# Moving half of the rounding of the activation codes into the attention's units

## The chip, the cores and the metric

The kernel runs on one core of one Trainium2 chip. The metric is the device time of one execution in microseconds (us), the median of the runs. The engines are PE (TensorE: matmuls; PEld is its weight load), DVE (VectorE), ACT (ScalarE), POOL (GpSimd) and SP (SyncE, which here only issues DMAs).

## What is computed

A decoder of two layers on x of 16 batches x 128 tokens x 256 channels. The change concerns the second layer's attention, whose queries, keys and values are computed from activations that have been scaled, clamped and rounded to FP8 codes:

```
def _div_clamp_fp8(x, scale):
    y = jnp.clip(x / scale, -448, 448)
    y = y.astype(bfloat16)
    return fp8_roundtrip(y)                       # the codes

q  = LN(codes(ln_out, q_in_scale)  @ wq)          # 16 heads of 128
k  = LN(codes(ln_out, k_in_scale)  @ wk);  v = codes(ln_out, v_in_scale) @ wv
core = softmax(q k / sqrt(d)) v
qx = LN(codes(ln_out, qx_in_scale) @ wqx); kx, vx from ctx_2048
xout = softmax(qx kx / sqrt(d)) vx
out = (codes(concat(core, xout), proj_smooth) @ wproj) * scales
```

So one input, ln_out, is rounded four times, once for each scale: for the queries, the keys, the values of the self attention, and for the queries of the cross attention.

## The kernel before, in words

All activations stay in SBUF. `XT` [128, 2, 2048] holds ln_out transposed: 2 blocks of 128 channels by 2048 tokens (16 batches of 128). `xq` [128, 4, 2, 2048] holds the codes: for each of four scales j (0 queries, 1 keys, 2 values, 3 cross) and each channel block k one *plane* of 2048 tokens.

`quant_layer` (L1464) does two things, one after the other, with a barrier of all engines between them.

`round_codes` (L1477) makes all eight planes, n = 4 x 2. Per plane ACT scales XT into bf16 (L1531, one instruction of 2048 columns), DVE clamps (L1549), takes the power of two out of it (L1554) and makes the rounding constant (L1562), each as two halves of 1024 columns; PE adds y + m - m in PSUM with three bf16 products per tile of 512 columns (L1521 to L1523), four tiles a plane; ACT copies two of the four tiles out (L1541) and DVE the other two (L1579). PE starts with three products of the identity (L1511).

`attention` (L1610) then works off 128 *units*: eight head groups w (four of self, four of cross attention) by 16 batches b, unit n = 16 w + b. The order of the work is written out by hand: each engine runs through the same steps, and in step s it does for each entry (stage, lag) of its list the stage of unit s - lag. Each engine's queue is in order, and semaphores tie them together. The lists are at L1830 (PE), L1907 (ACT), L1979 (POOL) and L2058 (DVE):

```
PE:   queries 0, keys_values 0, turn_p_warm 3, turn_q 1, turn_k 1, output 5, values 3, scores 1, late_output 5
POOL: rounded 5, row_deviation 7, deviation 0, prepare 0, context_low 0, normalise 2
DVE:  row_moments 6, apply_kv 1, maxima 2, query_statistics 0, clamp 4, key_statistics 0, power 4,
      magic 4, reciprocals 2, rounding 4, residual 5, apply_q 0
```

The loop that ties a unit to the next: PE computes queries and keys/values of unit u (L1731 to L1753) into one PSUM bank each; DVE takes their statistics (`query_statistics` L1992, `key_statistics` L1997); POOL adds an epsilon (L1947) and raises to the power -0.5 (L1952); DVE applies that to the queries (`apply_q` L2003) and keys/values (`apply_kv` L2010), which frees the banks; PE's queries of unit u+1 wait for `apply_q` of unit u. The other chains have one or more units of lag: scores (L1779), their maxima (DVE, L2017), exponentials (ACT, L1882), reciprocals (DVE, L2024), `normalise` (POOL, L1956), values (L1797), and the rounding of the result: scaled by ACT (L1899), `clamp`, `power`, `magic`, `rounding` on DVE (L2028 to L2043), `rounded` on POOL (L1963), then the output products (L1808) and DVE's `residual` (L2047).

`prepare` on ACT and POOL splits the weights of the next head group into a high and a low part: POOL has one such subtraction of 512 columns in the steps b = 5, 7, 9, 11 (L1423) and 10, 12 (L1432), and one of an expert's weights at b = 3 and 13 (L1940).

The attention keeps its normalised q, k, v and turned probabilities (`qn`, `kvn`, `pt`) in the space of XT, which nothing reads by then; so they appear as XT in the profile.

## Time and profile before

| | us |
|---|---|
| median of 3 runs | 1412.66 (1412.54 to 1413.17) |
| profiled execution, span | 1411.1 |
| PE busy | 1322.5 (94%) |
| DVE busy | 1073.4 (76%) |
| ACT busy | 944.4 (67%) |
| POOL busy | 909.4 (64%) |
| round_codes, first to last instruction | 341.9 to 370.8 |
| attention, first unit's products to the last unit's queries | 371.6 to 1121.6 |

The times of the runs are those of the whole execution; the profile gives one execution's span, from its first to its last instruction, with nothing of what lies around it. The profile places each instruction at a start with a duration. Shares of the whole span mix stages with different limits, so the stages named in the table are read each by itself.

### The profile page before, as it was taken

How to read it: one execution, taken by the hardware profiler on the slowest of the kernel's cores; microseconds unless marked ns; L12 is line 12 of the kernel's file. 1: busy time of each engine (PE TensorE's matmuls, PEld its weight loads, DVE VectorE, ACT ScalarE, POOL GpSimd, SP SyncE). 2: the span in 40 equal slices, each digit the busy share in tenths (PEclk: the TensorE clock that was granted, in tenths of full speed). 3: DMA queues.
4: the chain of work that ended last, by engine and by line, in shares of the span. 5: the costliest groups of instructions: out<-in, count | busy, mean ns of one | idle time of the engine just before them, and what ended most of it. 6: DMA issues, size and time to landing. Idle time of an engine off the chain costs nothing. (4 is left out here: it accounts for less than half of the span.)

```text
span 1411.1 us, 28423 instructions
## 1 busy us (share of the span) xinstructions
PE 1322.5 (94%) x8507; PEld 1098.8 (78%) x8507; DVE 1073.4 (76%) x2567; ACT 944.4 (67%) x3181; POOL 909.4 (64%) x1101
## 2 busy tenths in 40 slices
PE   9999988896799999999999999999999978999992
PEld 4445666663499999999999989998998855889882
DVE  5899768897788888888998888888888847444443
ACT  3997457776488787888887777777777746332331
POOL 4996237774178687786887767766867844455542
PEclk9999999998999999999999999999999999999996
DMA  9421110000101002002011020020100149577665
GB/s 341 158 117 63 36 46 2 1 2 1 60 1 62 29 2 98 1 31 69 24 61 53 1 91 2 1 91 2 46 1 24 68 144 340 138 168 162 164 162 134
DMA packets 55160, 105.85 MB, mean 75 GB/s; under 512 B 5052, under 2 KB 33668, under 8 KB 52708
## 3 DMA queue, kind: packets, MB, share of 16 engines
q1 hardware_dynamic: 46100, 84.90, 17.5%
q0 software_dynamic: 7488, 10.23, 4.5%
q10 hardware_dynamic: 1424, 8.91, 1.5%
q8 instruction: 73, 1.20, 0.4%
q14 instruction: 75, 0.61, 0.1%
HBM read 75.58 MB, written 28.44 MB: 74 GB/s over the span
## 5 line engine op out<-in xcount | busy, mean ns | idle before, releaser
L1882 ACT ACTIVATE pr_<-ps,neg_ 128x128 f32<-128x128 f32 x512 | 181.3, 366 | 64.5 <-DVE neg_ L2017 64.5
L1899 ACT ACTIVATE y<-ps,invsm 128x128 bf16<-128x128 f32 x512 | 146.4, 369 | 61.5 <-PE ps L1797 61.3
L1952 POOL TENSOR_TENSOR rstd<-var,half 128x6 f32<-128x6 f32 x128 | 172.3, 1346 | 10.1 <-POOL var L1947 0.2
L1963 POOL TENSOR_TENSOR z<-t,m 128x512 fp32r<-128x512 f32 x128 | 148.8, 1163 | 3.3 <-DVE t L2043 3.3
L1947 POOL TENSOR_TENSOR var<-stat,deps 128x6 f32<-128x6 f32 x128 | 26.0, 203 | 184.2 <-DVE stat L1997 184.2
L1779 PEld LDWEIGHTS ps<-qkt 128*128 128x128 f32 x1024 | 134.0, 191 | 10.3 <-ACT qkt L1866 2.7
L1808 PE MATMUL ps<-phi,z 128*128 128x256 f32 x512 | 138.2, 303 | 1.2 <-POOL z L1963 1.2
L1779 PE MATMUL ps<-qkt 128*128 128x128 f32 x1024 | 135.3, 275 | 2.3 <-ACT qkt L1874 2.1
L1797 PE MATMUL ps<-XT 128*128 128x256 f32 x512 | 131.8, 380 | 2.9 <-ACT XT L1890 2.8
L1956 POOL TENSOR_TENSOR pr_<-pr_,rec_ 128x512 f32<-128x512 f32 x128 | 133.5, 1043 | 1.4 <-DVE rec_ L2024 1.4
L1808 PE MATMUL ps<-plo,z 128*128 128x256 f32 x512 | 127.3, 279 | 0.0
L1992 DVE BATCH_NORM_STATS2 stat<-ps 128x6 f32<-128x256 f32 x256 | 97.7, 423 | 29.1 <-PE ps L1732 28.2
L2498 POOL DMA_INDIRECT sums<-f_ys,f_ids x39 | 61.8, 1585 | 88.7 <-PE ps L2354 43.4
L1731 PE MATMUL ps<-whi,xq 128*128 128x512 f32 x256 | 111.4, 435 | 4.7 <-DVE XT L2003 3.2
L1866 ACT ACTIVATE qkt<-ps,aff 128x512 f32<-128x512 f32 x128 | 99.0, 773 | 11.3 <-PE ps L1762 11.3
L1882 ACT ACTIVATION_READ_ACCUMULATOR pr_<-ps,neg_ 128x1 f32 x512 | 103.8, 203 | 0.0
L1732 PE MATMUL ps<-wlo,xq 128*128 128x512 f32 x256 | 100.8, 394 | 0.0
L1890 ACT ACTIVATE XT<-ps 128x512 f32<-128x512 f32 x128 | 76.5, 598 | 36.0 <-PE ps L1788 32.6
L2047 DVE SCALAR_TENSOR_TENSOR X<-ps,pscale,X 128x256 f32<-128x256 f32 x128 | 61.9, 484 | 47.8 <-PE ps L1808 47.6
L1808 PEld LDWEIGHTS ps<-phi,z 128*128 128x128 f32 x512 | 96.4, 188 | 2.2 <-POOL z L1963 1.7
L1808 PEld LDWEIGHTS ps<-plo,z 128*128 128x128 f32 x512 | 97.1, 190 | 0.1
L1797 PEld LDWEIGHTS ps<-XT 128*128 128x128 f32 x512 | 87.3, 189 | 11.2 <-ACT XT L1890 4.4
(357 smaller groups left out, 4023.8 us busy)
## 6 DMA issues: line engine op xcount, KB each, us to landing
f_w_low<-w_low SPq DMA_DIRECT2D x39, 512.0 KB, 3.6
centred<-raw_weights ACTq DMA_DIRECT2D x8, 1024.0 KB, 3.9
w_low<-w_dram SPq DMA_DIRECT2D x8, 1024.0 KB, 10.6
aw_st<-centred SPq DMA_DIRECT2D x7, 1024.0 KB, 6.1
raw_weights<-wself_dram SPq DMA_DIRECT2D x4, 1024.0 KB, 13.8
raw_weights<-wcross_dram SPq DMA_DIRECT2D x4, 1024.0 KB, 15.1
w_rest<-w_dram SPq DMA_DIRECT2D x8, 512.0 KB, 3.9
w_high<-w_top SPq DMA_DIRECT2D x8, 512.0 KB, 2.7
```

The lines of the kernel that those rows point to most:

```text
L1731: pe.matmul(bQ[:, :], x[:, k, :], whi[:, u.slot, 0, k, :], start=(k == 0), stop=False)
L1732: mm = pe.matmul(bQ[:, :], x[:, k, :], wlo[:, u.slot, 0, k, :], start=False, stop=(k == CB - 1))
L1779: mm = pe.matmul(bS[:, h * S:(h + 1) * S], qkt[:, u.par, h, :], qkt[:, u.par, HEADS + h // 2, :], start=True, stop=True)
L1797: mm = pe.matmul(bO[:, two], kvn[:, u.place, 2 + w, :], pt[:, u.par, two], start=True, stop=True)
L1808: mm = pe.matmul(bW[:, 0:C], z[:, u.par, h * S:(h + 1) * S], part[:, u.slot, h // 2, h % 2, :], start=(h == 0 and part is phi), stop=(h == ...
L1866: act.activation(qkt[:, u.par, 0:HEADS, :], bTQ[:, :].rearrange("p (h s) -> p h s", h=HEADS), ACT.Identity, bias=a[:, 1:2], scale=a[:, 0:1 ...
L1882: ins = act.activation(pr[:, u.par, h, :], bS[:, h * S:(h + 1) * S], ACT.Exp, bias=neg[:, u.par, h:h + 1], accum_out=tot[:, u.par, h:h + 1])
L1899: ins = act.activation(y[:, u.par, h * S:(h + 1) * S], bO[:, h * S:(h + 1) * S], ACT.Copy, scale=invsm[:, head:head + 1])
L1952: pool.tensor_tensor(rstd[:, u.par, 0:6], v, half[:, :], ALU.pow).then_inc(s_rstd, 1)
L1956: pool.tensor_tensor(pr[:, u.par, :, :], pr[:, u.par, :, :], rec[:, u.par, :].unsqueeze(2).to_broadcast([P, HEADS, S]), ALU.mult).then_inc ...
L1963: pool.tensor_tensor(z[:, u.par, :], t[:, u.par, :], m[:, u.par, :], ALU.subtract).then_inc(s_z, 1)
L1992: dve.bn_stats(stat[:, u.par, 6 * h:6 * h + 6], two)
```

## The change

Ahead of the attention `round_codes` now makes only the codes of self attention (three scales, six planes) and only of the first eight batches (1024 of 2048 columns, two tiles a plane). DVE's instructions there are 512 columns wide, and DVE and ACT copy out one tile each a plane.

The rest is cut into 20 *late pieces* of 512 columns. Pieces 0 to 5 are the six self planes of batches 8 to 11, pieces 6 to 11 those of batches 12 to 15; each of the units 0 to 11 has one. Pieces 12 to 19 are the cross codes of all batches, in the units 12, 16, ..., 40. A piece is a scaling on ACT, four instructions on DVE (`late_clamp`, `late_power`, `late_magic`, `late_rounding`, the last an addition of two tensors in SBUF) and one subtraction on POOL (`late_rounded`), one step later. PE has no part in a piece. PE's queries of unit 8 wait for six pieces, those of unit 12 for twelve, those of unit 64 for all.

The pieces are worked in buffers that are idle then (`raw_context`, `w2_top`), one each in turn; for that the first half of the first expert's weights is split at b = 12 instead of 3 in head group 0. XT must now live on: it lies on the right side of SBUF, the cross codes are written in its place (`xcross`), and `qn`, `kvn`, `pt` get a buffer of their own (`spare`).

```diff
-        xq = sbuf(ctx, "xq", [P, 4, CB, TOK], F32R)
+        xq = sbuf(ctx, "xq", [P, 3, CB, TOK], F32R)
         with ExitStack() as inner:
             round_codes(inner, xq, quant, **args)
 
-        attention(xq, row_stats, quant, rows_stored, w2_stored, **args)
+        columns_ctx.close()
+        xcross = sbuf(rows_ctx, "xcross", [P, CB, TOK], F32R, side="right")
...
-    N = 4 * CB
-    TILES = TOK // W512
+    N = 3 * CB
+    TILES = EARLY // W512
     BY_ACT = TILES // 2
...
+        def late(u, after):
+
+            at = u.n - after
+            i, off = (at, 0) if at < LATE_SELF else divmod(at + 3 * LATE_SELF, 4)
+            return i if off == 0 and 0 <= i < LATE else None
+
+        def late_place(i):
+
+            if i < LATE_SELF:
+                q, j = divmod(i, 3 * CB)
+                return j // CB, j % CB, slice(EARLY + q * W512, EARLY + (q + 1) * W512)
+            q, k = divmod(i - LATE_SELF, CB)
+            return CROSS, k, slice(q * W512, (q + 1) * W512)
...
-            return slice(0, I) if u.b == 3 else slice(I, 2 * I) if u.b == 13 else None
+            return slice(0, I) if u.b == (3 if u.w else 12) else slice(I, 2 * I) if u.b == 13 else None
...
+                    if u.n == EARLY // S:
+                        pe.wait_ge(s_late_z, 3 * CB)
+                    if u.n == (EARLY + W512) // S:
+                        pe.wait_ge(s_late_z, LATE_SELF)
+                    if u.n == SELF:
+                        pe.wait_ge(s_late_z, LATE)
...
+                    i = late(u, 0)
+                    if i is None:
+                        return
+                    if i >= 2:
+                        act.wait_ge(s_late_z, i - 1 if i < LATE_SELF else i)
+                    late_y, late_m, late_t = late_buffers(i)
+                    j, k, at = late_place(i)
+                    act.activation(late_y, XT[:, k, at], ACT.Copy, scale=quant.inv[:, j, k:k + 1]
...
-                in_steps([(turned_q, 2), (turned_k, 2), (prepare, 0), (context_high, 0), (scaled, 4), (row_normed, 8), (exps, 2),
+                in_steps([(late_scaled, 0), (turned_q, 2), (turned_k, 2), (prepare, 0), (context_high, 0), (scaled, 4), (row_normed, 8), (exps, 2),
...
+                def late_rounded(u):
+                    i = late(u, 1)
+                    if i is None:
+                        return
+                    j, k, at = late_place(i)
+                    late_y, late_m, late_t = late_buffers(i)
+                    pool.wait_ge(s_late_t, i + 1)
+                    pool.tensor_tensor(xcross[:, k, at] if j == CROSS else xq[:, j, k, at], late_t, late_m, ALU.subtract
+                                       ).then_inc(s_late_z, 1)
...
-                in_steps([(rounded, 5), (row_deviation, 7), (deviation, 0), (prepare, 0), (context_low, 0), (normalise, 2)])
+                in_steps([(rounded, 5), (row_deviation, 7), (late_rounded, 0), (deviation, 0), (prepare, 0), (context_low, 0), (normalise, 2)])
...
+                    dve.tensor_scalar(late_y, late_y, FP8_MAX, -FP8_MAX, ALU.min, ALU.max).then_inc(s_late_clamp, 1)
...
+                    dve.tensor_scalar(late_m.bitcast(U16), late_y.bitcast(U16), 0x7F80, None, ALU.bitwise_and
+                                      ).then_inc(s_late_p2, 1)
...
+                    dve.tensor_scalar(late_m, late_m, FP8_MIN_NORMAL, ROUND, ALU.max, ALU.mult).then_inc(s_late_m, 1)
...
+                    dve.tensor_tensor(late_t, late_y, late_m, ALU.add).then_inc(s_late_t, 1)
...
-                          (magic, 4), (reciprocals, 2), (rounding, 4), (residual, 5), (apply_q, 0)])
+                          (late_clamp, 0), (magic, 4), (late_power, 0), (reciprocals, 2), (late_magic, 0), (rounding, 4),
+                          (residual, 5), (late_rounding, 0), (apply_q, 0)])
```

What the tables do to the queues shows best in a unit in the middle of the first twelve. DVE, one unit of head group 0, from the maxima of one step to `apply_q`; before:

```order
L2017 TENSOR_REDUCE neg_<-ps 128x4
L1992 BN_STATS stat<-ps 128x6 x2
L2028 TENSOR_SCALAR y<-y 128x512
L1997 BN_STATS stat<-ps 128x6
L2034 TENSOR_SCALAR m<-y 128x512
L2039 TENSOR_SCALAR m<-m 128x512
L2024 RECIPROCAL rec_<-tot 128x4
L2043 TENSOR_TENSOR t<-y,m 128x512
L2047 SCALAR_TENSOR_TENSOR X<-ps,pscale,X 128x256
L2003 TENSOR_TENSOR XT<-ps,rstd 128x512
```

and in the changed kernel (its line numbers; the four rows on `raw_context` are the late piece):

```order
L2081 BN_STATS stat<-ps 128x6 x2
L2117 TENSOR_SCALAR y<-y 128x512
L2086 BN_STATS stat<-ps 128x6
L2123 TENSOR_SCALAR m<-y 128x512
L2047 TENSOR_SCALAR raw_context<-raw_context 128x512
L2128 TENSOR_SCALAR m<-m 128x512
L2055 TENSOR_SCALAR raw_context<-raw_context 128x512
L2113 RECIPROCAL rec_<-tot 128x4
L2064 TENSOR_SCALAR raw_context<-raw_context 128x512
L2132 TENSOR_TENSOR t<-y,m 128x512
L2136 SCALAR_TENSOR_TENSOR X<-ps,pscale,X 128x256
L2072 TENSOR_TENSOR raw_context<-raw_context 128x512
```

All four late instructions stand between the key statistics and `apply_q` (L2092, which follows), the addition last of all. POOL in the steps of units 11 and 12, with the weights' subtractions that are due there; before:

```order
L1947 TENSOR_TENSOR var<-stat,deps 128x6
L1952 TENSOR_TENSOR rstd<-var,half 128x6
L1423 TENSOR_TENSOR wlo<-aw_st,whi 128x512
L1956 TENSOR_TENSOR pr_<-pr_,rec_ 128x512
L1963 TENSOR_TENSOR z<-t,m 128x512
```

and in the changed kernel, to the start of unit 13:

```order
L2008 TENSOR_TENSOR rstd<-var,half 128x6
L1426 TENSOR_TENSOR wlo<-aw_st,whi 128x512
L2012 TENSOR_TENSOR pr_<-pr_,rec_ 128x512
L2019 TENSOR_TENSOR z<-t,m 128x512
L1971 TENSOR_TENSOR xq<-w_top 128x512
L2003 TENSOR_TENSOR var<-stat,deps 128x6
L2008 TENSOR_TENSOR rstd<-var,half 128x6
L1435 TENSOR_TENSOR plo<-aw_rows,phi 128x512
L1996 TENSOR_TENSOR w_rest<-w_rest,w_top 128x512
L2012 TENSOR_TENSOR pr_<-pr_,rec_ 128x512
L2019 TENSOR_TENSOR z<-t,m 128x512
L1971 TENSOR_TENSOR xcross<-raw_context 128x512
```

The piece's subtraction (L1971) stands behind `rounded` and ahead of the next unit's deviation; unit 12 has two subtractions of weights in one step, where before it had one.

## Rows read from the trace of the kernel before

**Rows 1.** Stretches: busy us (x instructions) of PE, PEld, DVE, ACT, POOL; clock; DMA
```profile
344.00:371.60 27.60, 23.68 (x100) 9.35 (x98) 25.60 (x63) 21.67 (x24) 0.19 (x3) 0.95 0.00 1
371.60:379.00 7.40, 4.37 (x22) 3.76 (x23) 3.25 (x7) 0.00 (x0) 1.55 (x2) 0.91 0.76 283
470.00:530.00 60.00, 60.00 (x444) 57.00 (x444) 52.27 (x125) 49.55 (x164) 46.32 (x49) 1.00 0.01 2
```

**Rows 2.** Timeline of round_codes: start, us, engine, line, instruction [idle before <-releaser]
```profile
346.78 0.43 PE L1523 MATMUL ps<-m,minus 128*128 128x512 bf16 x1
...
354.49 1.28 DVE L1579 CAST xq<-ps 128x512 fp32r<-128x512 f32 x2
355.69 0.75 DVE L1549 TENSOR_SCALAR y<-y 128x1024 bf16<-128x1024 bf16 x2
...
357.70 1.28 DVE L1579 CAST xq<-ps 128x512 fp32r<-128x512 f32 x2
...
369.50 1.34 DVE L1579 CAST xq<-ps 128x512 fp32r<-128x512 f32 x2 [0.68 <-PE ps L1523]
...
371.58 0.50 PE L1731 MATMUL ps<-whi,xq 128*128 128x512 f32 x1 [1.47 <-POOL deps L1915]
```

**Rows 3.** Timeline of one unit of the attention (b = 12), DVE, PE, then POOL
```profile
438.26 0.47 PE L1731 MATMUL ps<-whi,xq 128*128 128x512 f32 x1
440.40 0.43 DVE L1997 BATCH_NORM_STATS2 stat<-ps 128x6 f32<-128x256 f32 x1
440.75 0.28 DVE L2034 TENSOR_SCALAR m<-y 128x512 uint16<-128x512 uint16 x1
441.06 0.29 DVE L2039 TENSOR_SCALAR m<-m 128x512 bf16<-128x512 bf16 x1
441.27 0.17 DVE L2024 RECIPROCAL rec_<-tot 128x4 f32<-128x4 f32 x1
441.39 0.69 DVE L2043 TENSOR_TENSOR t<-y,m 128x512 f32<-128x512 bf16 x1
442.45 0.48 DVE L2047 SCALAR_TENSOR_TENSOR X<-ps,pscale,X 128x256 f32<-128x256 f32 x1 [0.37 <-PE ps L1808]
442.85 0.68 DVE L2003 TENSOR_TENSOR XT<-ps,rstd 128x512 f32<-128x512 f32 x1
443.92 0.47 PE L1731 MATMUL ps<-whi,xq 128*128 128x512 f32 x1
...
441.19 1.35 POOL L1952 TENSOR_TENSOR rstd<-var,half 128x6 f32<-128x6 f32 x1
442.51 1.27 POOL L1432 TENSOR_TENSOR plo<-aw_rows,phi 128x512 fp32r<-128x512 f32 x1
443.74 1.03 POOL L1956 TENSOR_TENSOR pr_<-pr_,rec_ 128x512 f32<-128x512 f32 x1
```

**Rows 4.** Timeline and instructions by line: DVE and POOL at one time
```profile
28.98 2.04 POOL L572 TENSOR_TENSOR kv<-ct 128x512 f32<-128x512 f32 x2
L272 DVE SCALAR_TENSOR_TENSOR n_shift<-n_mean_var,n_rstd x3: 129/164/1000, 29.0 to 137.4; 128x4 f32<-128x4 f32 x3
...
677.49 1.17 POOL L1963 TENSOR_TENSOR z<-t,m 128x512 fp32r<-128x512 f32 x1
677.86 0.94 DVE L2028 TENSOR_SCALAR y<-y 128x512 bf16<-128x512 bf16 x1
...
1130.23 0.66 DVE L2043 TENSOR_TENSOR t<-y,m 128x512 f32<-128x512 bf16 x1
1130.39 1.40 POOL L1956 TENSOR_TENSOR pr_<-pr_,rec_ 128x512 f32<-128x512 f32 x1 [0.55 <-DVE rec_ L2024]
...
L2043 DVE TENSOR_TENSOR t<-y,m x128: 660/693/694, 396.5 to 1145.0; 128x512 f32<-128x512 bf16 x128
```

**Rows 5.** Timeline of the attention's first unit
```profile
376.00 0.69 DVE L2003 TENSOR_TENSOR XT<-ps,rstd 128x512 f32<-128x512 f32 x1 [1.82 <-POOL rstd L1952]
...
376.75 0.50 PE L1731 MATMUL ps<-whi,xq 128*128 128x512 f32 x1 [3.03 <-DVE XT L2003]
```

More of the change, by code:

```diff
@@ L1529, in scaled @@
                     act.wait_ge(s_z, (n - 2) * TILES)
-                for h in (halves if n == 0 else [slice(0, TOK)]):
+                for h in (halves if n == 0 else [slice(0, EARLY)]):
                     act.activation(y[:, n % 3, h], XT[:, n % CB, h], ACT.Copy,
@@ L1655, in attention @@
         d_c = [sem(f"u_dc{k}") for k in range(4)]
+        s_late_y, s_late_clamp, s_late_p2, s_late_m, s_late_t, s_late_z = (
+            sem("u_late_" + n) for n in ("y", "clamp", "p2", "m", "t", "z"))
         names = ("cst", "chi", "clo", "q", "kv", "stat", "var", "rstd", "qn", "kvn", "tq", "tk", "qt", "kt", "sc", "neg",
@@ L1708, in load_context @@
                         sp.wait_ge(s_clo, b - 3)
+                    else:
+                        sp.wait_ge(s_late_z, LATE)
                     sp.dma_start(raw[:, b % 4, :, :], io["ctxT"].rearrange("(k p) n -> p k n", p=P)[
```

66 lines of the change are left out of this document (49 added, 17 removed).

## The prediction

> **What bounds the kernel now.** I read first the busy time by stretches, then the timeline of each of the two stages that the change touches. In the attention's steady stretch PE is busy for all of 60 us at the full clock, and DVE for 52.3 of them [rows 1]: PE sets the pace, with DVE close behind. In the rounding stage DVE is the busiest, 25.6 of 27.6 us [rows 1]. So the change takes work from a stage that DVE bounds and hands it to one in which DVE has about an eighth to spare.
>
> The timeline of one unit shows how little that is. Call K the start of the key statistics (440.40). `apply_q` starts at K+2.45, PE's next queries at K+3.52 [rows 3]. In the first unit, where PE only waits, queries follow `apply_q` by 0.75 (376.00 to 376.75) [rows 5], so they could start at K+3.20: the loop has 0.3 us in hand. DVE itself has a hole of 0.4 ahead of the residual: the rounding ends at 442.08, the residual starts at 442.45 [rows 3]. A unit takes 5.66 us (queries 438.26 to 443.92) [rows 3], and key statistics follow its queries by 2.14.
>
> **What the rounding stage gives back.** A plane costs DVE 3.21 us (354.49 to 357.70): two casts in 1.20, then six instructions of 1024 columns (two each for clamp, power, constant) in 2.01, or 0.335 each [rows 2]. With 512 columns an instruction of this kind starts 0.21 us after the one before (441.06 to 441.27) [rows 3], and a cast takes 0.61 until the next instruction starts (two of them 354.49 to 355.69). A plane becomes 6 x 0.21 + 0.61 = 1.87. The start does not shrink: PE runs its first products at half pace, and the second tile of plane 0 is done at 347.2 [rows 2]. From there DVE does cast 0 (0.61) and four times a plane with the cast before it (7.5): 355.3. The last tile then needs its three products and a cast, which ends at about 356.8. Before, the last cast ended at 370.84 [rows 2]. **Saved: 14.0 us** (12.5 to 15). The 0.75 us of barrier up to the first product (371.58) remain.
>
> **What a late piece costs.** The ACT scaling (about 0.6) and POOL's subtraction (1.17, as its twin in [rows 4]) lie beside other work; DVE's four instructions stand on the loop, between K and `apply_q`. In the queue order: power K+0.35, then at 0.21 each late clamp, magic, late power, reciprocal, then 0.12, late magic, 0.21, rounding at K+1.52, residual at K+2.13, late addition at K+2.53, `apply_q` at K+3.14. Interleaving hides the waits between dependent instructions and fills the hole, so 1.5 us of work would delay `apply_q` by only 0.7, and the queries by 0.7 - 0.3 = 0.4.
>
> But the late addition reads two tensors of SBUF, and there the trace shows something else. An addition of that kind on POOL and DVE hold each other up. POOL's subtraction of 677.49 ends at 678.66; DVE's bf16 clamp issued at 677.86 takes 0.94 instead of the 0.28 of its like at 440.75, and ends 0.15 after it. A two-tensor operation of four elements takes 1.00 instead of 0.13 at 29.0, beside a POOL instruction on two tensors that began at 28.98. The other way round, `normalise` issued at 1130.39, while the rounding's addition ran, takes 1.40 instead of 1.03 [rows 3, 4]. So who comes second waits for the end of the first, and then has all but 0.14 us of its own time before it. The Trainium skill (SBUF — State Buffer, Who interferes with whom) has this as a rule: DVE's second pair of ports is GpSimd's only one, held by an instruction with two SBUF inputs, or a bf16 tensor_scalar in its fast mode, to its end. The rows agree. It speaks against this change.
>
> Where the two meet: POOL is in the power function from K+0.79 to K+2.11, then in `prepare` or `normalise` (442.51) [rows 3]. The power function holds nobody up: the rounding's addition starts 0.2 us into it and takes 0.69, and in all 128 units it never took more than 0.694 [rows 3, 4]. The late addition, however, comes at K+2.53, when POOL has been in its next instruction for 0.4 us:
>
> - Plain unit: `normalise` ends at K+3.15; the addition at 3.15 + 0.55 = K+3.70; `apply_q` 0.08 earlier, queries at K+4.37 instead of 3.52. **+0.9** with the 0.1 that DVE is then late for the next statistics.
> - Unit with a weights' subtraction: that ends at K+3.38, the addition at 3.93. `normalise` now waits for it (to 4.83), then `rounded` (5.95) and the piece's subtraction (7.07). The next unit's clamp, which stands just ahead of its key statistics, would be due at K+6.5 and must wait for it: 7.22, and the key statistics start 0.08 before, at K+7.14 instead of 5.66. **+1.5**.
>
> The sum over the units:
>
> - 0 to 3: nothing. DVE waits there for POOL's power function between the statistics and `apply_q`, and the clamp chain of older units has not begun. If that cover were short: 0.2 each.
> - 4: no residual yet, the addition meets `normalise` head on; 0.3 if it wins, 1.2 if not: 0.8.
> - 5, 7, 9, 10 (with weights): 6.0. 6 and 8: 1.8.
> - 11: the queries of unit 12 wait for piece 11, whose subtraction ends at K+7.07; key statistics of unit 12 at K+9.27: 3.6. Queued behind this wait is everything of PE.
> - 12: two weights' subtractions and a piece; the clamp waits for `rounded`, the power for the piece's subtraction: 1.7, and 0.3 in unit 13 from POOL's late deviation.
> - 16, 20, 24, 32, 36, 40: 6 x 0.9 = 5.4; 28 (with weights): 1.2, as the following unit without a piece catches up.
> - The clock: PE idles 3 us in unit 0, and the granted clock of that stretch is 0.91, a part of it at 1.2 instead of 2.4 GHz [rows 1, 5]. The gap before unit 12 is as long; I take 0.6.
>
> Together **21.4 us**. The moved expert weights are in the unit-12 term; the extra DMA wait of the context (all pieces, done at unit 41) ends before its first use at unit 46, and costs nothing. Bounds: with no stop at all each piece costs 0.4, unit 11 3.2 and units 12 and 13 1.2 together, in all 10; if in addition POOL's power function is held up by the denser bf16 instructions ahead of it (by 0.13, the rest of a `magic`), everything shifts by that in 16 units: 23.5; with 1 us more of POOL backlog around units 9 to 13, 26.
>
> The profiled execution would go from a span of 1411.1 to 1411.1 - 14.0 + 21.4 = 1418.5; the median of the runs lies 1.6 above the span, so **1420.1**.
>
> **Rivals.**
>
> 1. *The order flips.* If POOL falls behind DVE, the late addition gets the ports first, and `normalise` waits instead. Then a piece costs 0.4, and only the clamps after units with weights are stopped (+0.6 each, four times). Cost 10 + 2.4 = 12.4: 1411.0, no change. For it: POOL's chain grows by 1.2 per unit. Against it: its power function starts on the statistics, which DVE itself delivers. Chance 0.12.
> 2. *The pieces are covered*, the other side. The pair of instructions does not collide, being bf16 to fp32 rather than fp32; each piece then costs 0.4, in all 10: 1408.7, faster. It decides if the stop is under 0.2 us a piece. The 1.40 of `normalise` beside just such an addition speaks against it. If the single pieces are absorbed too, 1406. Chance 0.13.
> 3. *Single pieces absorbed.* The eight later ones cost half, because the unit after catches up: cost 18, 1416.6. This is inside my forecast's range (1415 to 1425).
> 4. *The power function blocks as well.* It is a GpSimd instruction that reads SBUF, and all bf16 instructions issued after K+0.79 would wait for K+2.11: late power, late magic, rounding, residual and late addition follow then, 0.3 to 1.3 later than above, say 0.75 in 16 units: 12 more, 1432. The rows speak against it, as the rounding's addition runs through it unhindered [rows 3, 4]. Chance 0.05. The Trainium skill (SBUF — State Buffer, Who interferes with whom) says that whoever starts first holds the pair for the whole instruction, which read to the letter gives this rival; the 0.69 beside the power function disagrees.
> 5. The change does less than it says: no sign of it; the queues show all pieces.
>
> **How the numbers follow.** My forecast has the remaining 0.70. A measurement of this kernel tells about 0.2%, 2.8 us, from no change: 1409.8 to 1415.5. Faster: rival 2 and a little of rival 1: 0.15. Same: most of rival 1 and the low end of the forecast: 0.15. Slower: 0.70. The range leaves out rival 2 in part and rival 4: 1410 to 1427.
>
> **What would show it.** Right: the last cast near 356.8, the first product of the attention at 357.5; late additions of 1.2 to 1.5 us instead of 0.69 in units 5 to 11; clamps of about 1 us in units 6, 8, 10; query starts 6.5 to 7.2 apart in units 5 to 10 and 8.8 to 9.3 from 11 to 12. Wrong: late additions of 0.69 and `normalise` of 1.4 (rival 1), both at their old times (rival 2), late power or magic of over 1 us in the power function (rival 4), or a rounding stage that does not end before 358.

## The result and the profile after

The changed kernel takes **1428.45 us** (median of 4 runs, 1426.95 to 1429.68); the kernel before took 1412.91, measured beside it (4 runs, 1412.54 to 1414.62). The ratio is 1.0106, interval 1.0093 to 1.0118: slower by 15.5 us, where 7.4 were forecast; 1428.45 lies above the forecast's upper end of 1427. The profiled execution has a span of 1426.7 us, against 1411.1.

The times of one and the same kernel here differ by up to 10 us (e5 below), and a good part of that goes with a stretch of half clock in the routing stage behind the attention, whose instructions the change leaves alone (last section). So the kernels are compared mainly by stretches, each read from the one profiled execution of its kernel. The start of a unit is the start of its first query product, and the *distance* of a unit runs from there to the start of the next unit.

| us | first product | units 0 to 3 | 4 | 5 to 10 | 11 | 12 | 13 | 14 to 41 | 42 to 126 | last unit's queries to the end |
|---|---|---|---|---|---|---|---|---|---|---|
| before | 371.58 | 21.76 | 5.30 | 33.96 | 5.66 | 5.66 | 5.66 | 158.48 | 513.01 | 289.99 |
| after | 357.47 | 22.74 | 5.91 | 41.94 | 13.37 | 8.48 | 6.20 | 167.32 | 513.98 | 289.28 |
| difference | -14.1 | +1.0 | +0.6 | +8.0 | +7.7 | +2.8 | +0.5 | +8.8 | +1.0 | -0.7 |

The sum of the differences is the 15.6 us of the spans. The last column's 0.7 lies in stages whose instructions the change leaves alone.

The page of the changed kernel, its busy times:

```profile
span 1426.7 us, 28355 instructions
PE 1319.5 (92%) x8431; PEld 1096.0 (77%) x8447; DVE 1094.8 (77%) x2625; ACT 940.0 (66%) x3189; POOL 939.9 (66%) x1121
```

DVE has 21 us more than before and POOL 31. PE has 3 us less, which is a balance of two parts. Ahead of the attention it is busy for some 12 to 14 us less, mainly because 60 rounding products are gone (a few of its records are missing there). In the attention it is busy for 10.9 us more with the same number of products, in part at half clock. The attention's windows, of the kernel before and of the changed one:

```profile
371.58:1121.07 749.49, 743.81 (x5130) 1.00 0.10 37
357.47:1137.42 779.95, 754.73 (x5130) 0.99 0.10 35
```

The attention is 30.5 us longer, so 19.5 of them are PE's waits and 10.9 are products that last longer.

The windows of the changed kernel, with the columns of [rows 1]: the rounding stage, the attention's first unit, the surroundings of unit 11, and 60 us of units with single pieces:

```profile
344.00:357.00 13.00, 10.27 (x40) 4.18 (x39) 11.22 (x42) 9.00 (x12) 0.00 (x0) 0.92 0.01 1
357.47:364.87 7.40, 4.37 (x20) 3.71 (x21) 4.56 (x11) 1.84 (x3) 2.67 (x3) 0.89 0.75 283
425.00:445.00 20.00, 12.30 (x67) 10.69 (x67) 12.39 (x25) 9.76 (x33) 12.11 (x11) 0.83 0.00 1
456.00:516.00 60.00, 58.51 (x422) 54.27 (x423) 53.91 (x131) 46.95 (x157) 45.25 (x47) 1.00 0.15 54
```

In the third line PE works for 12.3 of 20 us at a granted clock of 0.83. In the last it is busy for 58.5 of 60 where [rows 1] had all 60.

**The rounding stage** ends as forecast. The timeline of the changed kernel (start, duration, engine, line, operation; in brackets the idle time before it and its releaser), last casts and first product of the attention:

```profile
354.62 0.68 DVE L1583 CAST xq<-ps 128x512 fp32r<-128x512 f32 x1
356.06 0.69 DVE L1583 CAST xq<-ps 128x512 fp32r<-128x512 f32 x1 [0.76 <-PE ps L1527]
357.47 0.50 PE L1766 MATMUL ps<-whi,xq 128*128 128x512 f32 x1 [1.46 <-POOL deps L1961]
```

The last cast ends at 356.75 (forecast 356.8), the first product starts at 357.47 (forecast 357.5).

**A late piece meets POOL**, as forecast. The timeline of the changed kernel around the late addition of 425.88, in a unit with a weights' subtraction (L2132 is the rounding's own addition, L2072 the late one, L2012 `normalise`, L2092 `apply_q`):

```profile
424.89 0.69 DVE L2132 TENSOR_TENSOR t<-y,m 128x512 f32<-128x512 bf16 x1
425.59 1.27 POOL L1435 TENSOR_TENSOR plo<-aw_rows,phi 128x512 fp32r<-128x512 f32 x1
425.88 1.53 DVE L2072 TENSOR_TENSOR raw_context<-raw_context 128x512 f32<-128x512 bf16 x1
426.82 1.49 POOL L2012 TENSOR_TENSOR pr_<-pr_,rec_ 128x512 f32<-128x512 f32 x1
427.33 0.68 DVE L2092 TENSOR_TENSOR spare<-ps,rstd 128x512 f32<-128x512 f32 x1
```

The rounding's own addition (L2132) takes 0.69. The late one (L2072), issued 0.29 us into POOL's subtraction, takes 1.53 and ends 0.55 after POOL's 426.86. Then `normalise`, issued while the late addition ran, takes 1.49 instead of 1.03, and `apply_q` (L2092), for which PE's next queries wait, starts at 427.33. All 20 late additions, by instructions of the line (count: shortest/median/longest in ns, first to last start):

```profile
L2072 DVE TENSOR_TENSOR raw_context<-raw_context x14: 684/1288/1529, 361.0 to 615.8; 128x512 f32<-128x512 bf16 x14
L2072 DVE TENSOR_TENSOR w_top<-w_top x6: 693/1516/1524, 367.3 to 433.1; 128x512 f32<-128x512 bf16 x6
```

Put beside POOL's timeline, 15 of the 20 start inside a POOL operation of 512 columns, and those take 1.28 to 1.53; the five that do not take 0.68 or 0.69. Four of these five stand in units 0 to 3. The fifth is that of unit 4, where it is `normalise` that is stopped:

```profile
384.48 0.68 DVE L2072 TENSOR_TENSOR raw_context<-raw_context 128x512 f32<-128x512 bf16 x1
384.58 1.48 POOL L2012 TENSOR_TENSOR pr_<-pr_,rec_ 128x512 f32<-128x512 f32 x1
```

**Unit 11** is where the forecast missed most. The timeline of the changed kernel, from piece 11's subtraction on POOL to unit 12's queries on PE:

```profile
436.61 1.15 POOL L1971 TENSOR_TENSOR xq<-w_top 128x512 fp32r<-128x512 f32 x1
437.80 0.72 ACT L1880 ACTIVATE raw_context<-XT,inv 128x512 bf16<-128x512 f32 x1 [6.51 <-POOL xq L1971]
438.42 0.76 ACT L1912 ACTIVATE qkt<-ps,aff 128x512 f32<-128x512 f32 x1
439.08 0.55 ACT L1920 ACTIVATE qkt<-ps,aff 128x256 f32<-128x256 f32 x1
439.74 2.05 PE L1814 MATMUL ps<-qkt 128*128 128x128 f32 x8 [6.61 <-ACT qkt L1912]
441.44 0.77 PE L1766 MATMUL ps<-whi,xq 128*128 128x512 f32 x1
```

And the waits of the same kernel from 430 to 442 us (what waited, for whom: total, times, longest):

```profile
PE ps L1814 <- ACT qkt L1912: 6.6, 1, 6.6
ACT raw_context L1880 <- POOL xq L1971: 6.5, 1, 6.5
DVE neg_ L2106 <- PE ps L1814: 6.0, 1, 6.0
```

PE does not wait first for its queries' codes. It waits for ACT: `late_scaled` of piece 12 (L1880) is the first entry of ACT's step, and it waits for twelve pieces, so for the end of piece 11 on POOL (`act.wait_ge(s_late_z, i - 1 if i < LATE_SELF else i)`). Its own buffer, `raw_context`, is free once piece 10 has ended; the wait for piece 11 guards `w2_top`, into which the weights' split of b = 12 writes later in the step. Behind it in ACT's queue stand the turned q and k of an older unit (L1912, L1920), for which the scores wait (L1814), and they stand ahead of the queries in PE's order. So the scores, 1.7 us, come after the wait rather than in it. In the granted clock the gap shows too: while PE idles it falls to the lower level, 1.2 GHz, at 438.3, and stays there to 445.2, where the 8 scores take 2.05 instead of 1.05 and the first query product 0.77 instead of 0.47 [rows 3].

### The profile page after: what moved, and what is told of

It is laid out like the page before. It is cut to its first block and busy times, and to the rows that moved or that the text cites. A ratio compares the mean times of both kernels' runs of the same rounds, so it can differ in the third digit from the quotient of the medians.

```text
span 1426.7 us, 28355 instructions
## 1 busy us (share of the span) xinstructions
PE 1319.5 (92%) x8431; PEld 1096.0 (77%) x8447; DVE 1094.8 (77%) x2625; ACT 940.0 (66%) x3189; POOL 939.9 (66%) x1121
## 5 line engine op out<-in xcount | busy, mean ns | idle before, releaser
L2019 POOL TENSOR_TENSOR z<-t,m 128x512 fp32r<-128x512 f32 x128 | 152.2, 1189 | 3.3 <-DVE t L2132 3.3
L1814 PEld LDWEIGHTS ps<-qkt 128*128 128x128 f32 x1024 | 133.7, 192 | 23.0 <-ACT qkt L1912 12.2
L1814 PE MATMUL ps<-qkt 128*128 128x128 f32 x1024 | 137.3, 277 | 10.7 <-ACT qkt L1912 7.9
L2012 POOL TENSOR_TENSOR pr_<-pr_,rec_ 128x512 f32<-128x512 f32 x128 | 136.4, 1066 | 1.4 <-DVE rec_ L2113 1.4
L1832 PE MATMUL ps<-spare 128*128 128x256 f32 x512 | 131.8, 379 | 2.8 <-ACT spare L1936 2.8
L1936 ACT ACTIVATE spare<-ps 128x512 f32<-128x512 f32 x128 | 76.5, 598 | 37.8 <-PE ps L1823 34.9
L1912 ACT ACTIVATE qkt<-ps,aff 128x512 f32<-128x512 f32 x128 | 99.0, 773 | 3.1 <-PE ps L1797 3.1
L2106 DVE TENSOR_REDUCE neg_<-ps 128x4 f32<-128x512 f32 x128 | 88.1, 688 | 15.9 <-PE ps L1814 9.7
L1832 PEld LDWEIGHTS ps<-spare 128*128 128x128 f32 x512 | 87.5, 188 | 11.3 <-ACT spare L1936 4.4
L1147 POOL TENSOR_TENSOR d_pr<-d_pr,rec 128x512 f32<-128x512 f32 x64 | 68.1, 1071 | 41.5 <-DVE rec L1335 41.0
L1280 ACT ACTIVATE d_pr<-ps,neg 128x128 f32<-128x128 f32 x256 | 89.4, 399 | 8.3 <-DVE neg L1326 8.3
## 6 DMA issues: line engine op xcount, KB each, us to landing
raw_weights<-wself_dram SPq DMA_DIRECT2D x4, 1024.0 KB, 13.7
```

The lines of the kernel that those rows point to most:

```text
L1280: ins = act.activation(pr[:, u.par, h, t, :], bS[h][:, t * P:(t + 1) * P], ACT.Exp, bias=neg[:, u.par, h, t:t + 1], accum_out=tot[:, u.par ...
L1814: mm = pe.matmul(bS[:, h * S:(h + 1) * S], qkt[:, u.par, h, :], qkt[:, u.par, HEADS + h // 2, :], start=True, stop=True)
L1832: mm = pe.matmul(bO[:, two], kvn[:, u.place, 2 + w, :], pt[:, u.par, two], start=True, stop=True)
L1912: act.activation(qkt[:, u.par, 0:HEADS, :], bTQ[:, :].rearrange("p (h s) -> p h s", h=HEADS), ACT.Identity, bias=a[:, 1:2], scale=a[:, 0:1 ...
L2012: pool.tensor_tensor(pr[:, u.par, :, :], pr[:, u.par, :, :], rec[:, u.par, :].unsqueeze(2).to_broadcast([P, HEADS, S]), ALU.mult).then_inc ...
L2019: pool.tensor_tensor(z[:, u.par, :], t[:, u.par, :], m[:, u.par, :], ALU.subtract).then_inc(s_z, 1)
```

## The experiments

The theories carry letters. **A**: in unit 11 ACT's scaling of piece 12 holds up everything behind it. Rival: PE's own wait for piece 11 sets the distance, whatever ACT does. **P**: late additions are stopped by POOL's 512-column operations, as both want two tensors from SBUF. Rival: DVE just has 1.5 us more to do in such a unit. **C**: the scaling at the head of ACT's step delays the turned q and k in the units with a piece, too. **K**: the stretch of half clock behind the attention follows from a short gap on PE there.

### Unit 11 and the ports: e1, e2, e3

e1 lets the scaling of piece 12 wait for piece 10 alone, the last one in its own buffer. The wait for piece 11 goes to the weights' split that needs it, and the split to b = 13:

```diff
-            return slice(0, I) if u.b == (3 if u.w else 12) else slice(I, 2 * I) if u.b == 13 else None
+            return slice(0, I) if u.b == (3 if u.w else 13) else slice(I, 2 * I) if u.b == (13 if u.w else 14) else None
...
-                        act.wait_ge(s_late_z, i - 1 if i < LATE_SELF else i)
+                        act.wait_ge(s_late_z, i - 1 if i <= LATE_SELF else i)
...
+                        if u.w == 0:
+                            act.wait_ge(s_late_z, LATE_SELF)
```

> Piece 12's scaling on ACT waits for eleven pieces instead of twelve, so that it no longer holds up what stands behind it in ACT's queue (the turned queries and keys of unit 10); the split of the first expert's weights moves from b = 12, 13 to 13, 14 and takes over the wait for twelve. Theory A (the 13.4 us from the queries of unit 11 to those of unit 12 are ACT's wait: PE's scores of unit 10 wait for ACT, which waits for piece 11, and only then come the queries): the distance falls to about 9.2, where PE's own wait for piece 11 binds; 1412.9 + 15.5 - 4 to 6 = about 1423. Rival B (PE's own wait for twelve pieces is what costs, and ACT's lies behind it): within 1 us of the changed kernel, 1427 to 1429, distance 12.5 or more.

e2 gives the late addition one input in PSUM (the bank of the queries) instead of the second one in SBUF. This kernel leaves the rounding constant out of the late codes; it is of use for its times alone:

```diff
-                    dve.tensor_tensor(late_t, late_y, late_m, ALU.add).then_inc(s_late_t, 1)
+                    dve.tensor_tensor(late_t, late_y, bQ[:, :], ALU.add).then_inc(s_late_t, 1)
```

> The changed kernel with the late addition reading one tensor in SBUF and one in PSUM (the queries' bank) instead of two in SBUF; this leaves the rounding constant's addition out of the 20 late pieces. Nothing else moves. Theory P (the two-tensor addition and POOL's normalise or weights' subtraction stop each other): late additions 0.69 us everywhere instead of 1.2 to 1.5, normalise back from 1.49 to 1.04 in the units with weights, query distances in units 5 to 10 from 6.95 to 6.1 to 6.4, single pieces from +1.2 to +0.7, in all 8 to 10 us off: about 1419. Rival D (DVE's own 1.5 us of added work is what costs, and the stops lie in time that would be waited anyway): distances within 0.2 of those of the changed kernel, 1426 to 1429.

e3 is both edits, and leaves out the same:

> Both edits of the two runs before together (and so again without the rounding constant's addition in the late pieces). If the two terms are apart, the savings add: 4 to 6 and 8 to 10, about 1414 to 1415, hardly above the kernel before. If unit 12's wait simply takes up what the units before it gain, it stays at 1418 or more.

Distances of the three, in the stretches of the first table:

| us | first product | 0 to 3 | 4 | 5 to 10 | 11 | 12 | 13 | 14 to 41 | 42 to 126 | to the end | median | ratio to before |
|---|---|---|---|---|---|---|---|---|---|---|---|---|
| after | 357.47 | 22.74 | 5.91 | 41.94 | 13.37 | 8.48 | 6.20 | 167.32 | 513.98 | 289.28 | 1428.45 | 1.0106 |
| e1 | 358.18 | 22.20 | 5.89 | 41.91 | 9.86 | 8.48 | 5.70 | 167.50 | 514.04 | 295.65 | 1431.46 | 1.0119 [1.0102, 1.0136] |
| e2 | 358.93 | 23.49 | 5.91 | 38.40 | 13.32 | 7.82 | 6.44 | 162.97 | 513.71 | 295.64 | 1428.01 | 1.0094 [1.0077, 1.0111] |
| e3 | 359.82 | 21.59 | 5.89 | 38.43 | 9.82 | 7.30 | 5.86 | 163.12 | 514.06 | 295.64 | 1417.91 | 1.0027 [1.0011, 1.0042] |

*e1.* The distance of unit 11 falls by 3.5 us. In the timeline the order has turned round: scaling and scores lie ahead of the wait, and PE waits for the codes themselves.

```profile
431.28 0.71 ACT L1880 ACTIVATE raw_context<-XT,inv 128x512 bf16<-128x512 f32 x1
433.22 1.13 PE L1814 MATMUL ps<-qkt 128*128 128x128 f32 x8
436.75 1.15 POOL L1973 TENSOR_TENSOR xq<-w_top 128x512 fp32r<-128x512 f32 x1
438.04 0.77 PE L1766 MATMUL ps<-whi,xq 128*128 128x512 f32 x1 [3.69 <-POOL xq L1973]
```

A holds for 3.5 of the 7.7 us, some 0.9 of them the scores at half clock (2.05 against 1.13 now). The edit also moves a split of weights out of unit 12. In ACT's step that split stands behind the turned q and k, so it has no part in the 3.5; whether the 0.5 us less in unit 13 come from it was not tested. The other 4.2 are PE's wait for piece 11 itself, the rival's part, which the forecast priced at 3.6. The queries still meet the lower clock (0.77), behind a wait of 3.7 us. As a whole, however, the kernel was not faster: 1431.5 against 1428.5. From the last queries to the end it took 6.4 us longer, in a stage that this edit does not touch.

*e2.* Late additions on `raw_context`, by line (of all 20, 15 again start inside a POOL operation of 512 columns, and none takes over 0.69):

```profile
L2072 DVE TENSOR_TENSOR raw_context<-raw_context,ps x14: 676/678/689, 362.4 to 610.3; 128x512 f32<-128x512 bf16 x14
```

With one input in PSUM none is stopped. Units 5 to 10 save 3.5 us, units 14 to 41 4.4 and unit 12 0.7: 8.6 us are due to the stops, and P holds. A single piece's own unit takes 5.99: of its 0.93 the stop is 0.60, and 0.33 are left. It is not the whole price of the pieces: of the 8.0 and 8.8 us in units 5 to 10 and 14 to 41 some 4.5 are left in each. Again 6.4 us came on top behind the attention, so the median, expected at 1419, is no lower than the changed kernel's.

*e3.* The savings add up stretch by stretch: units 5 to 10 as in e2, unit 11 as in e1. The profiled execution again has the long end (295.64); the runs lie apart, at 1415.6 to 1418.2 (six, granted clock 0.981 or 0.982) and 1421.8 to 1424.2 (four, 0.977 to 0.980).

### The place of the scaling: e4

e4 is e1 with the scaling further back in ACT's step:

```diff
-                in_steps([(late_scaled, 0), (turned_q, 2), (turned_k, 2), (prepare, 0), (context_high, 0), (scaled, 4), (row_normed, 8), (exps, 2),
+                in_steps([(turned_q, 2), (turned_k, 2), (prepare, 0), (context_high, 0), (late_scaled, 0), (scaled, 4), (row_normed, 8), (exps, 2),
```

> The first run's kernel with ACT's scaling of a late piece behind prepare and context_high in ACT's list instead of at its head, so that it is no longer ahead of the turned queries and keys that PE's scores wait for. Theory C (the 0.24 us by which the unit before each single piece is longer, and part of the 1.0 us in units 0 to 3, are this scaling on ACT): the units 15, 19, 23 ... go back from 5.90 to 5.68, 2 to 3 us off the first run. Rival: these 0.24 us come from DVE or POOL, no change against the first run.

1422.73 us (1421.34 to 1423.54), ratio 1.0053 [1.0036, 1.0070]; 6.6 of the 8.7 us below e1 are the stretch to the end (289.06), which the edit does not touch. In the changed kernel the unit before each single piece has a distance of 5.90 instead of 5.66; the timeline of one, its ACT and PE:

```profile
464.38 0.60 ACT L1936 ACTIVATE spare<-ps 128x512 f32<-128x512 f32 x1
464.87 0.71 ACT L1880 ACTIVATE raw_context<-XT,inv 128x512 bf16<-128x512 f32 x1
465.49 0.77 ACT L1912 ACTIVATE qkt<-ps,aff 128x512 f32<-128x512 f32 x1
466.81 1.13 PE L1814 MATMUL ps<-qkt 128*128 128x128 f32 x8
```

The scaling stands between the copy of the turned probabilities and the turned q, and puts the latter off by 0.62 (464.87 to 465.49). PE has some slack, and 0.24 of it reaches the scores. In e4 the same distance is 5.66. Units 14 to 41 take 165.84, 1.7 us less than e1's, which is seven times 0.24; C holds. Unit 3 gained as well (5.91 in e1, 5.31), but units 1 and 2 lost more. Unit 12 went from 8.48 to 7.54, which says nothing of the scaling: the stretch of half clock at its start lasts 3.4 us in e4 and 6.8 in e1.

### One instruction a unit, or five: e5, e6, e7

These three leave the self codes to the rounding stage (six planes of 2048 columns) and move the eight pieces of cross codes alone, with ACT's scaling at e4's place. e5 spreads the work of a piece over several units, by tables of unit numbers, and puts the addition ahead of the rounding (the cut shows it against the kernel before):

```diff
+EARLY = TOK
+LATE = CB * NTG
+ACT_AT = [0, 4, 8, 14, 18, 22, 30, 34]
+CLAMP_AT = POWER_AT = [1, 5, 9, 15, 19, 23, 31, 35]
+MAGIC_AT = [2, 6, 10, 16, 20, 24, 32, 36]
+ADD_AT = [3, 7, 11, 17, 21, 25, 33, 37]
+SUB_AT = [5, 9, 15, 18, 23, 31, 34, 39]
...
-                          (magic, 4), (reciprocals, 2), (rounding, 4), (residual, 5), (apply_q, 0)])
+                          (late_clamp, 0), (magic, 4), (late_power, 0), (reciprocals, 2), (late_magic, 0), (late_rounding, 0),
+                          (rounding, 4), (residual, 5), (apply_q, 0)])
```

> Another way to move codes: all self codes ahead of the attention, only the cross codes late, in eight pieces; each piece is spread over four to ten units (scaling on ACT in its hole ahead of the scaled values; clamp and power one unit later, constant in the next, addition in the next and there ahead of the rounding's own, where POOL is in the power function; subtraction on POOL in a unit that follows one without weights). Theory P (a piece costs only what it pushes past the slack of the loop or into the stops with POOL): query distances stay at 5.66 to 5.75 in units 5 to 45, the rounding stage is two planes shorter, 2 x 3.2 = 6.4 us, in all 5 to 6.4 us under the kernel before: about 1407.5. Rival D (a piece costs DVE's and POOL's time wherever it stands, 1.2 us each): 8 x 1.2 - 6.4 = 3 us over the kernel before, about 1416.

e6 has all of a piece's ACT and DVE work in one unit, with the late addition in its place of the changed kernel (against e5):

```diff
-ACT_AT = [0, 4, 8, 14, 18, 22, 30, 34]
...
+ACT_AT = CLAMP_AT = POWER_AT = MAGIC_AT = ADD_AT = [4, 8, 14, 18, 22, 30, 34, 38]
...
-                          (late_clamp, 0), (magic, 4), (late_power, 0), (reciprocals, 2), (late_magic, 0), (late_rounding, 0),
-                          (rounding, 4), (residual, 5), (apply_q, 0)])
+                          (late_clamp, 0), (magic, 4), (late_power, 0), (reciprocals, 2), (late_magic, 0), (rounding, 4),
+                          (residual, 5), (late_rounding, 0), (apply_q, 0)])
```

> The same eight cross pieces in the same homes, but each whole in one unit (4, 8, 14, 18, 22, 30, 34, 38) with the addition behind the residual, as the changed kernel has it, and ACT's scaling in its hole. Theory P: the addition stops at normalise, each piece costs 0.9 to 1.0: 7 to 8 us, less 6.4, so 1413 to 1415. Rival D: the same as the spread kernel to 1 us.

e7 is e6 with the late addition ahead of the rounding, as in e5:

> The dense kernel with the late addition ahead of the unit's own rounding (and of the residual) instead of behind them. Theory P: the late addition then runs within POOL's power function and is not stopped (0.69 us), but the rounding's own addition is pushed to the moment at which normalise starts (K+2.1), so one of the two is stopped: between the dense and the spread kernel, a piece 0.4 to 0.9, 1409.5 to 1414. If only the place of a two-tensor addition against POOL's 512-column instructions counts, exactly the additions that start within them are longer than 0.7 us, in all three kernels of this call.

| us | first product | 0 to 3 | 4 | 5 to 10 | 11 to 13 | 14 to 41 | 42 to 126 | to the end | a unit with a piece | median |
|---|---|---|---|---|---|---|---|---|---|---|
| e5 | 364.93 | 21.93 | 5.33 | 33.97 | 16.98 | 158.48 | 513.65 | 290.92 | 5.66 | 1415.83 (1407.71 to 1417.58) |
| e6 | 365.42 | 24.09 | 5.60 | 34.97 | 16.98 | 164.49 | 513.92 | 296.29 | 6.59 | 1421.56 (1415.82 to 1423.49) |
| e7 | 366.50 | 21.59 | 6.60 | 35.36 | 16.98 | 166.88 | 513.93 | 296.66 | 6.99 | 1425.08 (1420.23 to 1426.71) |

The late additions of the three, in this order:

```profile
L2059 DVE TENSOR_TENSOR raw_context<-raw_context x8: 659/660/686, 384.2 to 576.4; 128x512 f32<-128x512 bf16 x8
```

```profile
L2056 DVE TENSOR_TENSOR raw_context<-raw_context x8: 683/1290/1291, 393.8 to 592.6; 128x512 f32<-128x512 bf16 x8
```

```profile
L2056 DVE TENSOR_TENSOR raw_context<-raw_context x8: 691/692/693, 391.9 to 593.6; 128x512 f32<-128x512 bf16 x8
L2116 DVE TENSOR_TENSOR t<-y,m x128: 660/693/1558, 392.5 to 1151.8; 128x512 f32<-128x512 bf16 x128
```

In e5, eight pieces cost nothing in the units that hold them: 158.48 us for units 14 to 41, the same to the hundredth as before, while the first product of the attention comes 6.65 us earlier. In e6, with the same instructions in one unit and the addition behind the residual, a unit with a piece costs 0.93, and seven of eight additions are stopped at 1.29: the single piece's price in the changed kernel (6.59) is reproduced.

e7 was expected between the two and came out dearer than e6, 1.33 a piece. Its late addition is in fact not stopped (0.69). But it and the three others put off the unit's own rounding addition (L2116), which now meets `normalise`: it takes up to 1.56, eight times out of 128, each issued 0.03 us into `normalise`. The stop has moved to a neighbour, and it is longer, 0.87 instead of 0.60: 0.27 of the 0.40 by which a piece is dearer than in e6. So what counts is not which of the instructions comes first but that DVE has issued both additions before POOL leaves the power function, and with 1.5 us more in one unit it cannot.

The medians tell less than the stretches: e5's 12 runs fall into 1407.7 to 1409.7 (four, granted clock 0.982 to 0.984) and 1415.0 to 1417.6 (eight, 0.977 to 0.980). Its ratio, 1.0003 [0.9987, 1.0019], is a mean over the two. The expected whole times (1407.5, 1413 to 1415, 1409.5 to 1414) hold for e5's lower group alone; e6 and e7 have 5.4 and 5.7 us more behind the attention than e5, and with these taken off e6 is still above its range.

### The end of the kernel, and a version that beats both: e8, e9, e11

e8 is e5 with four short products without effect (the identity by itself into an idle bank) at each of two places of the routing stage where PE otherwise waits; e9 is the kernel before with the same eight:

```diff
+FILL = 4
...
+                for _ in range(FILL):
+                    pe.matmul(bH[:, 0:2 * P], ident[:, :], ident[:, :].unsqueeze(1).to_broadcast([P, 2, P]), start=True, stop=True)
```

> The spread kernel with four products of the identity (of 2 x 128 columns, result unused) ahead of each of two waits of PE in the routing stage, where PE was idle for 2.2 to 2.5 us. Theory K (in some executions the granted clock falls to half for 13.7 us just as PE works the 64 products of the map and the weights' splits, which costs 6 us of the 1415 to 1417 that the spread kernel often took; what PE did before decides it): the stretch from the last unit's queries to the end is 289 to 291 us in the profile and the runs lie near 1407.5 throughout, 5 to 6 under the kernel before. Rival: the half clock is not bound to these gaps, the runs stay in two groups, 1408 and 1416.

> The kernel before with the same eight products. Both theories: it met the half clock in this stage for 3.4 us only, so nothing to gain: within 1.5 us of the kernel before.

e8: 1408.77 us (1407.85 to 1412.75, nine runs), ratio 0.9966 [0.9956, 0.9976]; the upper group of e5 does not occur. e9: 1415.15 (1413.09 to 1419.22), ratio 1.0007 [0.9997, 1.0017]. The kernel before gains nothing; its end takes 291.06 us with the products, 289.99 without, in one profile each. This fits K but does not show it: e5 and e8 ran at different times and on different chips, and the waits do not decide by themselves (last section).

e11 puts the findings together. Twelve batches are rounded ahead (three tiles of a self plane), the six self pieces of batches 12 to 15 and the eight cross pieces are late, their instructions spread, each subtraction where POOL has no weights' one, the wait of e1 and the products of e8. The cut, against the kernel before, leaves out how the waits and buffers follow from the tables:

```diff
+EARLY = 3 * W512
+LATE_SELF = 3 * CB
+LATE = LATE_SELF + CB * NTG
+ACT_AT = [0, 1, 2, 3, 4, 6, 8, 14, 17, 20, 24, 30, 33, 36]
+CLAMP_AT = POWER_AT = [0, 1, 2, 3, 5, 7, 9, 15, 18, 21, 25, 31, 34, 37]
+MAGIC_AT = [0, 1, 2, 3, 5, 7, 9, 15, 18, 21, 25, 31, 34, 37]
+ADD_AT = [0, 1, 2, 3, 6, 8, 10, 16, 19, 22, 26, 32, 35, 38]
+SUB_AT = [1, 2, 3, 4, 7, 9, 15, 17, 21, 23, 31, 33, 37, 39]
```

> The spread kernel, further: the six self pieces of batches 12 to 15 are late too, four whole in the units 0 to 3 and two spread over 4 to 9, the cross pieces spread from unit 8 on with clamp, power and constant in one unit and the addition in the next; with the eight products. Theory P: units 0 to 3 hide a whole piece (DVE waits there for POOL's power function), a unit has room for three bf16 instructions (0.63) or one addition (0.61), none of them beside POOL's 512-column work: query distances as before to 0.1 us, rounding stage 3 us shorter than the spread kernel's, about 1404. Rival: three instructions in one unit are over the slack: 0.3 us for each of ten pieces, 1407.

**1402.82 us** (1400.38 to 1404.64, five runs), ratio 0.9916 [0.9903, 0.9930]: 11 us faster than the kernel before (1413.99 beside it). First product at 360.91, 10.7 us earlier; units 0 to 3 20.66, 4 to 13 56.32, 14 to 41 158.76, 42 to 126 513.71, end 292.57. So fourteen pieces cost units 4 to 41 0.4 us in all. Units 0 to 3 are 1.1 shorter, in a profile without half clock there. The end is 2.6 longer than before, though its half clock lasts 3.4 us in both; that stays open. No run tells which of e11's parts the 11 us need, the eight products among them. Its late additions:

```profile
L2077 DVE TENSOR_TENSOR raw_context<-raw_context x11: 659/662/693, 364.4 to 577.1; 128x512 f32<-128x512 bf16 x11
```

## Why the prediction was right and wrong

That the kernel becomes slower was forecast, and for the right reason. The size was not: the attention lost 30.5 us instead of 21.4.

**Right: what bounds the two stages, and the saving.** 14.0 us forecast, 14.1 measured, with both marks (356.8 and 357.5) within 0.1.

**Right: the stop.** "Late additions of 1.2 to 1.5 us instead of 0.69" came as 1.28 to 1.53, and the query distances of units 5 to 10 lie between 6.87 and 7.25, their sum 8.0 us over before where 7.8 were forecast. Counted as the forecast counts, from key statistics to key statistics, units 5, 7, 9 and 10 take 7.24 to 7.26 (forecast 7.14), 6 and 8 6.62 and 6.63 (forecast 6.56). e2 shows the mechanism by taking it away; without the stop a piece costs its unit 0.33, where 0.4 was forecast. Clamps in the units 6, 8 and 10 were forecast at about 1 us and took only 0.73 or 0.74; they too end 0.15 us after POOL's subtraction.

**Luck: unit 4.** The term of 0.8 was a middle between 0.3, if the late addition comes ahead of `normalise`, and 1.2. It cost 0.6. The addition did come ahead, by 0.1 us, so this part is the 0.3; the other 0.3 is the scaling of unit 5's piece (unit 4 takes 5.91, in e4 5.60), which the sum had left out.

**Right: rival 4 falls.** The late power and magic, issued while POOL was in the power function, took 0.28 to 0.30. By the Trainium skill (SBUF — State Buffer, Who interferes with whom) whoever issues first has the shared pair for the whole instruction, so they should have waited. For this POOL instruction the trace disagrees. Rivals 1 and 2 fall too: no late addition issued inside a POOL operation of 512 columns ran in 0.69, and the order that rival 1 needs occurred in unit 4 alone; and no piece from unit 4 on was covered. Rival 3 falls, as the unit after did not catch up (5.69 in unit 17).

**Wrong: "11: the queries of unit 12 wait for piece 11 ... 3.6".** The term costs only PE's wait, and that was nearly right: 4.2 in e1. The unit cost 7.7. What failed is the sentence ahead of the sum, that the ACT scaling lies "beside other work". In unit 12 it has a wait of its own, for piece 11, and stands at the head of ACT's step. The prediction asked what is queued behind PE's wait, and did not ask it of ACT's. This cost 3.5 us (13.37 to 9.86 in e1), the scores at half clock among them.

**Mis-sized: the clock.** Taken at 0.6 for unit 11's gap, by the likeness to unit 0's gap of 3 us; PE idled 6.6. The half clock lasted 6.8 us: the scores cost 1.0 more, and unit 12's queries and keys/values, which take 3.56 us instead of 1.94 (438.26 to 440.20 before), another 1.6, most of it in the distance of unit 12. That covers what units 12 and 13 cost above forecast (3.4 instead of 2.0). With 3.4 us of half clock, in e4, which has the stops, they cost 1.9.

**Mis-sized: single pieces, 8.8 instead of 6.6.** The pieces' own units cost 0.93 (forecast 0.9). What was missed is the unit before: 0.24 for the scaling, seven times, 1.7 in all, by e4. This is the same sentence on ACT that failed. The rest is 0.02 us in each of the other units, of which below.

**Missed: units 0 to 3, 1.0 instead of 0,** and **units 42 to 126, 1.0 instead of 0.** For the first there is the scaling in unit 3 (5.89, in e4 5.31), but unit 1 alone lies anywhere from 5.1 (e3) to 7.75 (e6), with a stretch of half clock that comes now sooner, now later, and lasts 3.4 to 10.2 us where there is one. In e3 and e11 no half clock falls into these units, and unit 1 takes 5.10 and 5.09; the kernel before has 3.4 us of it there and 6.22. It stays open what each part costs. The second is 0.01 to 0.02 us in each of 85 units without a piece, with nothing that waits. All kernels with the new places in SBUF have 0.6 to 1.05 of it, e5 too, and e9, with the old ones, has none. That points to the places, but no run moved these alone, and they do not set the size, which differs between kernels with the same places (0.64 in e5, 0.91 in e6).

Where the sum went by DVE and POOL, whose queues were followed instruction by instruction, the saving and units 5 to 10 were right to 0.2 us; where ACT was costed by a phrase, 5.2 us were missing (3.5 and 1.7), of the 9.1 by which the attention's 30.5 exceed the 21.4. The rest is mainly the half clock in units 12 and 13 and the two terms that stay open.

## What to carry to other kernels

When a stage is cut up and put into the slack of a steady loop, cost each piece on every engine by its place in the queue: the wait that it brings, what stands behind that, and who needs it within the step. Total slack says little: here eight pieces with five instructions in one unit cost 0.93 us each, and the same instructions spread over several units cost nothing. And a wait that guards something used late in a step belongs just ahead of that use, not at the step's head, where it holds a whole queue. With the scaling behind the turned q and k, the addition ahead of POOL's next operation and the work spread, moving a smaller part of the codes (e11: 14 pieces instead of 20, and with it the eight products) went with 11 us less, where the changed kernel lost 15.

## What was not expected of the hardware

**A stretch of half clock of 3.4 or of 13.7 us, in a stage that was not changed.** It begins 41 to 43 us after the last unit's queries in the kernel before, the changed kernel, e5, e8, e9 and e11 and lasts 3.4 (6.8 in e5), in e4 after 49 us for 3.4; in the profiles of e1, e2, e3, e6 and e7 it begins at about +57 and lasts 13.7 (e2 has one of 3.4 at +40 as well). PE's windows of e6 (stretch, PE busy, granted clock, DMA share, GB/s), then of e8 and of before:

```profile
1180.00:1185.00 5.00, 3.96 (x24) 0.73 1.04 401
1185.00:1190.00 5.00, 5.00 (x25) 0.50 1.03 410
1190.00:1195.00 5.00, 5.00 (x21) 0.50 0.50 194
```

```profile
1170.00:1175.00 5.00, 4.70 (x37) 1.00 1.04 402
1175.00:1180.00 5.00, 5.00 (x39) 1.00 1.02 405
```

```profile
1175.00:1180.00 5.00, 3.97 (x31) 1.00 1.05 398
1180.00:1185.00 5.00, 5.00 (x41) 1.00 1.02 407
```

In the slice in which the map's products start PE is equally busy in e6 and in the kernel before (3.96 and 3.97 of 5 us), and the DMA share is the same, so neither tells the two apart. At the lower level 25 products fit into 5 us instead of 39 to 41. The map's products, in e6 and in e5:

```profile
L2405 PE MATMUL ps<-f_router,X x64: 275/421/423, 1181.0 to 1193.4; 128*128 128x78 f32 x64
```

```profile
L2408 PE MATMUL ps<-f_router,X x64: 275/275/307, 1171.7 to 1178.9; 128*128 128x78 f32 x64
```

They stand right behind a wait of PE. In e6, with the idle time in brackets:

```profile
1173.41 0.46 PE L2398 MATMUL ps<-f_router 128*128 128x128 f32 x2 [2.17 <-DVE f_router L2619]
1181.04 12.80 PE L2405 MATMUL ps<-f_router,X 128*128 128x78 f32 x64 [2.47 <-POOL f_router L2552]
```

e1, e3 and e7 have the same two waits to 0.03 us, and the kernel before only 0.5 to 1.3 there. But the length of a wait does not decide: e2 has the long stretch behind a wait of 1.25,

```profile
1186.03 11.88 PE L2421 MATMUL ps<-f_router,X 128*128 128x78 f32 x64 [1.25 <-POOL f_router L2568]
```

and e4 has the first of the two waits, 2.18, and 3.4 us of half clock alone.

From the first to the last of the 64 products it is 12.4 us in e6 and 7.2 in e5, a difference of 5.2, nearly all of the 5.4 by which e6's end is longer than e5's. By their times, executions of one and the same kernel fall on either side (e5, e3), and with a few small products in PE's gaps (e8) none of nine runs fell into e5's upper group. What decides between the two in an execution, and whether the kernel before, whose profile shows the short one, ever has the long one, stays open.

**Who is stopped gets a part back.** The second of two such instructions does not take POOL's rest plus its own time: issued 0.29 us into a subtraction of 1.27 us, the late addition took 1.53, not 0.98 + 0.69 = 1.67, as if the first 0.14 us of it had run already. This is the 0.14 of [rows 4], and it holds for DVE's and for POOL's instruction (`normalise` at 426.82: 1.49, 0.90 of them after the late addition's end).

**Which POOL instruction stops DVE is not a matter of its being there.** In the changed kernel the power function of POOL (128x6, 1.34 to 1.46 us) is running when the rounding's addition starts in 123 of 128 units, and that takes 0.68 to 0.70, so it is not stopped. POOL's addition of the same size ahead of it (128x6, 0.20 us) does stop: 16 late clamps issued 0.03 to 0.04 us into it end 0.15 us after it and take 0.31 or 0.32 instead of 0.28. Why the one and not the other, no run here shows.
